# Message-passing layer on one core: a register fetch moved ahead of four instructions, and a sum written straight as whole numbers

## The reference: what is computed

```python
h = relu(layernorm(x)); x = x + log_softmax(mean_over_edges(h[src]) @ W_l.T + h @ W_r.T + b)
h = relu(layernorm(x))
weight = relu(edge_attr @ W1 + b1) @ W2 + b2          # E x 128
msg = (h @ Wl + bl)[src_or_dst_column] * weight       # msg = h[col] * weight
x = x + segment_sum(msg, row, num_segments=N)
```

## Time and profile before

| | |
|---|---|
| median of 3 runs | 3461.39 us (3461.23, 3461.39 and 3470.03) |
| span of the profiled execution | 3469.3 us |
| busy: PE, DVE, ACT, POOL | 2987.6, 2757.6, 2085.3, 1808.5 us |
| mean granted TensorE clock | 0.959 |

### The profile page before, as it was taken

One profiled execution on the slowest core, in us unless ns is written; L12 is line 12 of the kernel. 1 busy time (PEld: TensorE's weight loads), 2 busy tenths in 40 slices (PEclk: granted clock), 3 DMA queues, 4 the chain that ended last, 5 costly groups with the idle time before them and its releaser, 6 DMA issues.

```text
span 3469.3 us, 97235 instructions
## 1 busy us (share of the span) xinstructions
PE 2987.6 (86%) x26330; PEld 2437.6 (70%) x26331; DVE 2757.6 (79%) x7718; ACT 2085.3 (60%) x4907; POOL 1808.5 (52%) x1790
## 2 busy tenths in 40 slices
PE   0799999999668878899999989988889898998977
PEld 0699999999655556776766666766667666766766
DVE  8899999999786657777777777777777777777866
ACT  2599999998353335555555545555455555555656
POOL 3400010000127777667766676666766677677750
PEclk9999999999868889999999999999999999999999
DMA  3198888960103336666666656655666666666657
GB/s 117 37 326 313 311 309 310 311 213 3 38 19 107 103 103 172 179 175 160 178 164 161 160 150 172 166 162 147 166 168 180 165 158 184 173 158 175 181 154 207
DMA packets 506188, 593.04 MB, mean 171 GB/s; under 512 B 71050, under 2 KB 477058, under 8 KB 505905
## 3 DMA queue, kind: packets, MB, share of 16 engines
q1 hardware_dynamic: 449506, 470.49, 49.4%
q0 software_dynamic: 56400, 119.07, 9.9%
HBM read 293.94 MB, written 295.35 MB: 170 GB/s over the span
## 4 chain that ended last, share of the span: by engine, by line
DVE 36%; PE 32%; issue 17%; DVEq 7%; DMA 4%; POOL 2%; ACT 1%; SPq 0%; POOLq 0%; ACTq 0%
PE PS L1119 11%; DVE X L1017 8%; PE PS L1110 5%; DVE big L990 4%; PE PS L1282 4%; PE PS L1249 4%; DMA messages<-big,idxr 4%; DVE big L978 3%; DVE aux L768 3%; DVEq L1012 3%; DVE big L964 2%; DVE big L975 2%; DVE big L967 2%; DVE hpar L1006 2%; PE PS L1261 2%
## 5 line engine op out<-in xcount | busy, mean ns | idle before, releaser
L605 POOL DMA_INDIRECT messages<-big,idxr x1664 | 1637.0, 984 | 720.8 <-issue 466.5
L1282 PE MATMUL PS<-big,hpar 128*128 128x128 f32 x5120 | 663.8, 283 | 163.7 <-DVE hpar L1006 128.7
L1282 PEld LDWEIGHTS PS<-big,hpar 128*128 128x128 f32 x5120 | 610.5, 195 | 223.1 <-DVE hpar L1006 181.2
L1432 ACT ACTIVATE big<-PS,b1c 128x512 f32<-128x512 f32 x416 | 286.0, 688 | 708.3 <-PE PS L1238 708.3
L1017 DVE TENSOR_TENSOR X<-X,PS 128x128 f32 x1280 | 368.7, 288 | 325.3 <-PE PS L1282 131.9
L1119 PE MATMUL PS<-h_parts,counts 128*128 128x258 f32 x3626 | 565.3, 296 | 0.0
L1359 ACT ACTIVATE counts<-PS 128x784 fp32r<-128x784 f32 x592 | 481.7, 825 | 93.9 <-PE PS L1110 85.6
L1249 PE MATMUL PS<-W2s,big 128*128 128x128 f32 x3328 | 500.8, 295 | 0.0
L1249 PEld LDWEIGHTS PS<-W2s,big 128*128 128x128 f32 x3328 | 419.0, 197 | 98.3 <-issue 98.3
L1119 PEld LDWEIGHTS PS<-h_parts,counts 128*128 128x128 f32 x3626 | 470.2, 191 | 0.2 <-ACT counts L1359 0.2
L1443 ACT ACTIVATE big<-PS 128x512 f32<-128x512 f32 x416 | 247.6, 595 | 347.2 <-PE PS L1261 339.4
(11 more groups left out here) (222 smaller groups left out, 3639.1 us busy)
## 6 DMA issues: line engine op xcount, KB each, us to landing
messages<-zeros SPq DMA_DIRECT2D x896, 193.5 KB
big<-messages SPq DMA_DIRECT2D x320, 516.0 KB
aux<-slot_rows SPq DMA_DIRECT2D x416, 128.0 KB
big<-in_edge_attr_dram SPq DMA_DIRECT2D x402, 128.0 KB
messages<-big,idxr POOLq DMA_INDIRECT x1664
X<-in_x_dram SPq DMA_DIRECT2D x12, 448.0 KB, 6.9
out_dram<-X SPq DMA_DIRECT2D x6, 448.0 KB
edge_places<-big SPq DMA_DIRECT2D x1, 2496.0 KB, 13.2
```

The costliest lines, as they stand in the source:

```text
L605: pool.indirect_dma_start(strm_d, bass.IndirectOffsetOnAxis(ap=idxr[:, n % U, j:j + 1], axis=0), outr[:, n % U, j, :], None).then_inc(S_sc ...
L1282: last = nc.tensor.matmul(to[:, r * C:(r + 1) * C], finhot[:, n % 2, r * 2 + q, :], fin[:, k, r, q * ROW:q * ROW + C], start=(q == 0), sto ...
```

## The change

Two edits in DVE's program for layer 1, and the semaphore values that follow from them:

1. The sum L980 writes `idxr` (int32) itself. L984 and `place_f` go. The wait for the scatter of four steps ago stands ahead of the sum now. `rank_chain` counts 4 instead of 5 for each step; POOL (`scatter`) and ACT (`local_rows`) wait for the third of them (the sum), where they waited for the fifth.
2. The register load and its address arithmetic (L1012, L1013) become `pair_places`, called between `messages` and `row_places`; `block_adds` gets the addresses. In `segment` and behind the last step it is still called right ahead of `block_adds`.

```diff
@@ row_places
-                wait(dve, S["rank_chain"], g * 5)
+                wait(dve, S["rank_chain"], g * 4)
...
-                nc.vector.tensor_reduce(place_f, place[:, 1, :, :], AX, ALU.add).then_inc(S["rank_chain"], 1)
+                dve.wait_ge(S["rank_chain"], g * 4 + 2)
+                wait(dve, S_sc[k], (g - k) * 16)
+                with nc.allow_low_precision(reason="one whole number below 2 ** 24 in each sum"):
+                    nc.vector.tensor_reduce(idxr[:, k, :], place[:, 1, :, :], AX, ALU.add).then_inc(S["rank_chain"], 1)
                 nc.vector.tensor_tensor(taken, taken, pQ[:, J, :], ALU.add).then_inc(S["rank_chain"], 1)
-                dve.wait_ge(S["rank_chain"], g * 5 + 3)
-                wait(dve, S_sc[k], (g - k) * 16)
-                nc.vector.tensor_copy(idxr[:, k, :], place_f).then_inc(S["rank_chain"], 1)
@@ octave additions
-            def block_adds(i, sums):
+            def pair_places(i):
                 dve.load(pair_regs, bq_i[0:1, ds(i * (FO // 2), FO // 2)])
-                ats = [dve.snap(pair_regs[r], min_val=0, max_val=(NB - 1) * C) for r in range(FO // 2)]
+                return [dve.snap(pair_regs[r], min_val=0, max_val=(NB - 1) * C) for r in range(FO // 2)]
+
+            def block_adds(i, sums, ats):
                 dve.wait_ge(S["finmm_done"], i + 1)
@@ layer1
                 messages(s, n)
+                if adding[0]:
+                    last = o[0] - 1 if o else adding[0][0]
+                    ats = pair_places(last)
                 if more:
                     row_places(s + 1, n + 1)
                 if adding[0]:
-                    block_adds(o[0] - 1 if o else adding[0][0], pFL[adding[0][1] % 2])
+                    block_adds(last, pFL[adding[0][1] % 2], ats)
@@ scatter (POOL), local_rows (ACT), ranks (PE)
-                    pool.wait_ge(S["rank_chain"], 5 * g + 5)
+                    pool.wait_ge(S["rank_chain"], 4 * g + 3)
-                act.wait_ge(S["rank_chain"], g * 5 + 5)
+                act.wait_ge(S["rank_chain"], g * 4 + 3)
-                wait(pe, S["rank_chain"], g * 5)
+                wait(pe, S["rank_chain"], g * 4)
```

More of the change, by code:

```diff
@@ L227, in gnn_program @@
         taken = part(big, used, NBK)
-        place_f = part(big, used, J)
         away = part(big, used, FO // 2 * P).rearrange("p (t v) -> p t v", t=FO // 2)
@@ L594, in scatter @@
                     pool.wait_ge(S["rank_chain"], placed)
-                    pool.reg_add(placed, placed, 5)
+                    pool.reg_add(placed, placed, 4)
                     pool.wait_ge(S["lrow_ready"], lrows)
@@ L609, in _ @@
                 scatter(g, g)
-            pool.reg_mov(placed, 5 * U + 5)
+            pool.reg_mov(placed, 4 * U + 3)
             pool.reg_mov(lrows, U + 1)
@@ L973, in row_places @@
                 dve.wait_ge(S["rank_done"], g + 1)
-                wait(dve, S["rank_chain"], g * 5)
+                wait(dve, S["rank_chain"], g * 4)
                 nc.vector.tensor_tensor(place[:, 0, :, :], pQ[:, 0:J, :], taken.unsqueeze(1).to_broadcast([P, J, NBK]), ALU.add)\
                     .then_inc(S["rank_chain"], 1)
-                dve.wait_ge(S["rank_chain"], g * 5 + 1)
+                dve.wait_ge(S["rank_chain"], g * 4 + 1)
                 nc.vector.tensor_tensor(place[:, 1, :, :], place[:, 0, :, :], hotW[:, s, 1:, :], ALU.mult).then_inc(S["rank_chain"], 1)
-                dve.wait_ge(S["rank_chain"], g * 5 + 2)
-                nc.vector.tensor_reduce(place_f, place[:, 1, :, :], AX, ALU.add).then_inc(S["rank_chain"], 1)
+                dve.wait_ge(S["rank_chain"], g * 4 + 2)
+                wait(dve, S_sc[k], (g - k) * 16)
+                with nc.allow_low_precision(reason="one whole number below 2 ** 24 in each sum"):
+                    nc.vector.tensor_reduce(idxr[:, k, :], place[:, 1, :, :], AX, ALU.add).then_inc(S["rank_chain"], 1)
                 nc.vector.tensor_tensor(taken, taken, pQ[:, J, :], ALU.add).then_inc(S["rank_chain"], 1)
-                dve.wait_ge(S["rank_chain"], g * 5 + 3)
-                wait(dve, S_sc[k], (g - k) * 16)
-                nc.vector.tensor_copy(idxr[:, k, :], place_f).then_inc(S["rank_chain"], 1)
             def messages(g, n):
@@ L1033, in layer1 @@
                 if adding[0]:
-                    block_adds(o[0] - 1 if o else adding[0][0], pFL[adding[0][1] % 2])
+                    block_adds(last, pFL[adding[0][1] % 2], ats)
                 adding[0] = o
             def next_part(p):
-                dve.wait_ge(S["rank_chain"], 5 * TURN[p - 1])
+                dve.wait_ge(S["rank_chain"], 4 * TURN[p - 1])
                 link(nc.vector.tensor_copy(taken[:, 0:NB], starts[:, p, 0:NB]))
@@ L1045, in _ @@
             steps(dve, layer1, next_part)
-            block_adds(OCT0[-1] - 1, pFL[(OCT0[-1] - 1) % 2])
+            block_adds(OCT0[-1] - 1, pFL[(OCT0[-1] - 1) % 2], pair_places(OCT0[-1] - 1))
             def segment(i, n):
@@ L1050, in segment @@
                     stream_hot(i + 1, n + 1)
-                block_adds(i, pF[:, n % 4, :])
+                block_adds(i, pF[:, n % 4, :], pair_places(i))
             stream_hot(OCT0[-1], 0)
```

## The result

The changed kernel takes 3304.8 us (median of 4 runs, 3301.4 to 3311.6) against 3461.3 us (3459.8 to 3470.0): a ratio of 0.954, with an interval of 0.9522 to 0.9558. It is 156 us faster, where 123 were forecast; 3304.8 lies between the forecast and rival 5 (3296). Of the profiled execution the span falls from 3469.3 to 3305.3 us.

The account below looks back on a forecast made before the run. VectorE was taken to bound looped steps with an octave, PE those without, GpSimd as the stage's floor. The raw 145 us less 3, 15 and 5 gave about 123 saved: 3461.4 to 3338 us, 8-in-10 range 3304 to 3408.

Parts of the forecast that it names:

- rival 5: Whole kernel: all of it and more, nothing exposed behind L990, GpSimd's floor reached; 3296 us, chance 0.04.
- The cause of the hole: VectorE's 0.69 us hole ahead of the additions (L1017) comes from the register load and address arithmetic, not L1282.
- rival 2: Ahead of L1017 the additions do wait for L1282; net 30 us saved, 3431 us, chance 0.06.
- Saved ahead of L1017: Looped step, L981 to L1017: L984 and the load go, 0.31 us is left, 0.66 us saved.
- Exposed behind L990: The moved load makes L990 to L975 0.80 us instead of 0.60: 0.20 us exposed, bounds nothing and 0.87.
- A looped step: VectorE's looped step with an octave falls by 0.49 us, from 5.92 to 5.43 us.
- Raw sum: 240 looped steps at 0.49 us and 43 written-out ones at 0.64 us: 145 us saved before losses.
- The next engine's room: The new 5.43 us step barely fits PE's 5.32 and GpSimd's 5.14; PE's limit in parts 2 and 3 takes 3 us.
- rival 1: The next engine takes part: looped steps stop at 5.6 us by PE's waits; 82 us saved, 3380 us, chance 0.18.
- GpSimd: Its growing backlog, with blocked steps at part borders, costs 15 us, and SP's wait for last scatters 5 us.
- Steps without an octave: PE sets these 3.90 us steps, so nothing is gained; if PE did not, 11 us.
- Rival 3: The load waits until L990 has ended, L975 comes 0.87 us later; 50 us more, 3511 us, chance 0.08.

Follow-up runs that it names:

- e3: Changed kernel with the fetch issued later, inside the row places behind L974 and the wait on `rank_chain` for it; 3428.7 us, ratio 0.9892.
- e10: Kernel before the change with three instead of four scatters in each step (output incomplete, for times alone); 3387.4 us, ratio 0.9768.
- e7: Changed kernel with three instead of four scatters in each step (output incomplete, for times alone); 3187.5 us, ratio 0.9181.
- e1: Kernel before the change with only the fetch moved behind `messages`, the cast kept; 3382.6 us, ratio 0.9746.
- e2: Changed kernel with the fetch put back right ahead of the additions, so only the cast is gone; 3384.2 us, ratio 0.9753.
- e11: Changed kernel with the four places fetched by four loads of one register each instead of one load of four; 3603.6 us, ratio 1.0382.
- e5: Changed kernel with part 4's loop cut into turns of 8 steps instead of 16, same work; 3301.3 us, ratio 0.9516.

## Why the prediction was right and wrong

- **The cause of the hole**: right. It was the load and not L1282; rival 2 is out (after the change 5.6 us of idle ahead of L1017 are ended by it in the whole execution, 131.9 before).
- **Saved ahead of L1017**: too small. I expected 0.31 us to be left and 0.66 saved; 0.12 is left and 0.85 saved. My 0.31 took the address and its waits to start behind the row's sum. The queue had them done before.
- **Exposed behind L990**: this is the step that failed. I read the earlier trace rows as "the load starts when the instruction ahead of it starts" and took 0.20 us; it was nothing in 145 of 240 looped steps and 0.14 us in the other 95, 0.05 on the mean. What the earlier trace rows show is the other case of the same rule. In the tail each addition of L1017 waits by `fadd_done` for the one before it; the last one starts at 3382.21, the fetch's register instruction at 3382.34 and its load at 3382.45, just behind the start of L1006, so the last unmet wait was the last addition's. In most looped steps L988's wait was met, and the load ran one instruction earlier, under L1004. The bound "nothing" was in the range, but with too little weight. The Trainium skill, "Perfetto Trace Analysis", section "DVE / Act Engine Instruction", has the sequencer free for the next instruction once one is pushed, and the semaphore wait behind that. Here the trace agrees for a met wait (load at 1490.1, L988 at 1490.40). Behind an unmet wait it is different: in the kernel before the load starts at 1512.51, only when the waiting cast has started (1512.39), and in e3 the fetch behind a wait for the engine's own last result cost 0.65 us a step. Whether such a wait is pushed with its instruction or stands in the queue by itself, no run shows.
- **A looped step**: 5.43 forecast, 4.98 to 5.07 found. Raw sum: 145 forecast, about 200 found, which is what the parts shrink by when GpSimd has room (2228.9 to 2030.5, e10 to e7). It is not evenly spread: parts 1, 4, 5 and 6, with 144 of the looped steps with additions, give 142 us, and parts 2 and 3, with 96, only 52.
- **The next engine's room**: TensorE's 5.32 was mis-sized. I had taken only the wait shown out of a step of 5.85 us; without any wait it is at most 5.06, so 0.26 us more of that step was slack. That kept rival 1 (3380) out and the step's room open. In parts 2 and 3 the term was too small the other way: I took 3 us for TensorE's share, and with room at GpSimd a looped step with additions gains about half a microsecond there, beside nearly one elsewhere.
- **GpSimd**: right in kind (blocked steps between the loops, growing tail) and too small: 15 + 5 us forecast, some 40 found. I take the error to follow from the first, which no run tests by itself: a step at 5.0 us is below GpSimd's 5.05, so in the parts with an octave in every step it recovers nothing between the borders; at my 5.43 it would have recovered 0.3 us a step. The two errors are of opposite sign, and it is luck that the total missed by 33 us and not by 55.
- **Steps without an octave**: I put them at nothing, since VectorE waits for TensorE in them. They went from 3.91 to 3.82 us; in part 0, with three scatters, 53 steps gain 4.0 us (205.8 to 201.8). The likely reason is that `ranks` on TensorE waits for VectorE's `rank_chain`, which is now complete one instruction sooner; e1, which keeps the cast, stays at 3.91, and e2, which drops it, is at 3.82.
- **The sum into int32**: right, 361 ns for 361 before. **The moved wait**: no cost of it is seen apart from GpSimd's; no run has it alone.
- **Rival 3**, the load not hidden, did not occur in the change, and e3 shows that its mechanism is real one instruction further down, behind an unmet wait. **Rival 5** had the mechanism nearly whole, nothing exposed and GpSimd's floor reached, and came within 9 us. It had 0.04.

## What to carry to other kernels

In all these kernels a register load costs what lies between the last wait that is unmet when the queue gets there and the instruction that uses the register. So put it ahead of the waits on the engine's own results, and count from the wait, not from the neighbouring instruction. When a step is cut below the period of an engine that used to catch up in it, its backlog stays: compute that engine's own floor and let the new step run against it, because that is where the gain ends. An engine that waits for nothing is not thereby the bound; take some of its work away and see. And when two kernels differ by more than their steps do, compare the lengths of the same part: here 34 of the 46 us by which e1 missed lay in the four turns of one loop.

## What the runs showed of the hardware

L959 (128x512, `tensor_scalar`; L958 after the change) takes 0.35 us, but up to 0.56 when it starts about half a microsecond into a GpSimd scatter. Timeline of e1, both engines, two steps:

```profile
1477.98 1.00 POOL L605 DMA_INDIRECT messages<-big,idxr  x1 [0.30 <-issue]
...
1478.37 0.35 DVE L959 TENSOR_SCALAR big<-aux,iotaP 128x512 bf16<-128x512 int16 x1
1478.63 0.68 DVE L1006 TENSOR_TENSOR hpar<-iotaN,big 128x512 f32<-128x512 f32 x1
...
1483.23 0.95 POOL L605 DMA_INDIRECT messages<-big,idxr  x1 [0.30 <-issue]
...
1483.74 0.54 DVE L959 TENSOR_SCALAR big<-aux,iotaP 128x512 bf16<-128x512 int16 x1
1484.20 0.67 DVE L1006 TENSOR_TENSOR hpar<-iotaN,big 128x512 f32<-128x512 f32 x1
...
1484.49 1.22 POOL L605 DMA_INDIRECT messages<-big,idxr  x1 [0.30 <-issue]
```

At 0.39 us behind the scatter's start it takes 0.35 us, at 0.51 us behind it 0.54; the next instruction starts 0.46 instead of 0.26 us later, and the next scatter takes 1.22 us. Over all steps its mean is 391 ns in e1, 367 before and 372 after. It is 0.2 of the 0.3 us by which some steps of e1 are longer than their neighbours of 5.24, but only part of e1's miss: 416 x 24 ns are 10 of the 46 us. That the two engines wait for each other here is argued from the times, not shown. The Trainium skill, "SBUF — State Buffer", section "Terms", says that VectorE and GpSimd share one port pair, which one of them locks for the whole of an instruction, with the other blocked. The trace does not bear out a lock for the whole scatter: at 1478.37 L959 starts and ends inside a scatter of 1.00 us and takes its usual 0.35. A lock for a part of the scatter would fit, and no run here separates that from another cause.

The loops of 16 steps in parts 2, 3 and 4 stop for 3.5 to 6 us at each turn, with VectorE, TensorE or both waiting for nothing that the profile shows ("issue"); those of 8 steps stop for about 1 us, but for 6 to 7 us in part 1 of e1 and in parts 5 and 6 of e11. e5 shows that the longer stop is on the path. The traces show what goes with it: packets on the two queues of the kind "instruction". From the DMA view of the four turns of part 1, first in e1 (1380 to 1600 us), then in the changed kernel (1375 to 1555 us); packets, MB, share:

```profile
q14 instruction: 22, 0.18, 0.3%
```

```profile
q14 instruction: 2, 0.02, 0.0%
```

Part 5 of e11 has 21 such packets (2940 to 3175 us). In part 4 (2435 to 2670 us) the changed kernel has 23 on q8 and 19 on q14; e5, whose loop there is half as long, has one on each (2450 to 2670 us). Part 0, whose loop of 16 steps has no octaves, has neither such stops nor such packets in its turns. So the stops come where a turn brings instructions in again; that the one causes the other is argued from this, not shown. e1 and e11 differ from their neighbours in VectorE's program alone, and it is q14 that is busy in their long turns. Why the same 8 steps need it in one part of one kernel and not in the others stays open; no run changes the length or the place of a loop's code alone. A stop also costs more than itself: in e1 TensorE is idle for 7 us up to 1409.4, comes back at a granted clock of 0.50 (1.2 GHz) until 1413.3, and its 16 matmuls of L1287 take 3.78 us instead of 2.05.
